# A batch-by-batch attention stage and an expert stage on one core: side work placed inside the first products, and the second product's tiles placed between the next unit's first products

## The chip, the cores and the metric

The kernel runs on one core of a Trainium2 chip. The metric is the device time of one execution in microseconds, less is better. The engines are named as in the profile: PE (TensorE) with its weight loads (PEld), DVE (VectorE), ACT (ScalarE), POOL (GpSimd) and SP (SyncE), each with its own queue of instructions, worked off in order.

## What is computed

For 16 batches of 256 positions and 256 channels (f32) the reference runs three residual blocks, each followed by a layer norm:

```python
x = layernorm(x + linear_recurrence(x))              # scan over positions, then a 256x256 product
x = layernorm(x + cross_attention(x, ctx))           # 16 heads of 16, rotary, window of 50
# experts:
probs = softmax over positions of (silu(h @ router_w1) @ router_w2).T      # 16 experts
weights, token_indices = top_k(probs, 64)            # each expert picks 64 positions of every batch
gate  = silu(picked @ w1[e]);  value = picked @ w2[e]
out   = (gate * value) @ w3[e]                       # scaled by the weights, scatter-added per batch
x = layernorm(x + combined)
```

Each expert has 256 channels in, 512 hidden (`FF`) and 256 out.

## The kernel before

The program has two blocks, each with an instruction stream per engine written out by hand, with semaphores between them.

**`mixing`** runs the recurrence, the attention and the router for one batch after another. A step of the pipeline (`step(it)`) has 16 slots `t`, one for each head; other stages of neighbouring batches are put into given slots. Step 15 is the last with heads; step 16 is a drain, with the last output projections. What matters here is the end: PE's output projection of batch 14 (`O`, L692) needs `attnT`, whose second half POOL makes in `inverse_sums(it, -1)` (L481 to L488) from ACT's `rough` (L826). In step 15 POOL also takes the first unit's token rows: it waits for `route.placed` (DVE, `place_picked`, L153), copies indices (L541) and issues four indirect DMAs (L545). PE turns these rows in step 16 (L726). After the projection come DVE's statistics (L953 to L962), ACT's estimate (L159, L161), POOL's refinement (L167 to L175), DVE's normalised rows `x2cur` (L969), PE's transposes (L657), ACT's copy `x2T` (L856), the router's first product (L740) and the last weighted sum of the attention (L636). All engines go to the second block together.

**`experts`** handles 32 units: 16 experts times two halves of the batches, each with four tiles of 128 rows (`CB` = 4, a tile holds the 64 picks of two batches). All products are split in three for accuracy (hi·hi, hi·lo, lo·hi in fp32r), so a unit costs PE:

- `up`: for each of four `f` tiles of the hidden size, six 128x512 products into `gate_bank` and six into `value_bank` (L1342). A bank pair alternates, so `f` waits for gate and hidden of `f - 2`.
- `turn`: eight transposes of the next unit's rows (L1352), which ACT and DVE split into `xT_hi` and `xT_lo` (`columns`).
- `down`: for four tiles `m`, twelve 128x256 products each into `y_bank` (L1342, `attn` in the trace), for the unit before. A bank pair alternates again.

Some names: `gate_of` (ACT, L1465), `multiply` (DVE, L1560), `h_high` (ACT, L1469), `h_low` (DVE, L1552) make the hidden operand; `split` (ACT L1452, DVE L1542) the weights; `weigh` (ACT, L1479) scales each output tile `y`; `gather` (POOL, L1265) fetches rows two units ahead; `scatter` (POOL, L1283) adds `y` to `acc_rows`, each tile after the same tile of the unit before has landed.

The last batch's rest is handled in the first units, with single-unit additions: `project_O` in unit 0, `normalise_O` (DVE, L1615) at the end of unit 2, `turn_x2` (PE, L1401), ACT's copy `x2T` (L1502), `route_x2` (L1408) and the copy to `r1` (L1513) in unit 3 (`LATE - 1`), POOL's preparation of `rw2_placed` (L1299, L1306), the logits (L1430) and `find_maximum` (L1644) in unit 4 (`LATE`), the turned picks (L1438) and `place_picked` (L153) in unit 10. PE's order in a unit is:

```python
turn_x2 (unit 3);  up(it);  turn(it.step(1));  side work of this unit, and its wait;  down(it.step(-1))
```

At the end DVE, ACT and POOL normalise the last four accumulators (`statistics(c)`, L1567; `normalise(c)`, L1578), each after its last scatter and a load.

Of the kernel before, what the change touches and what calls it, by code (L numbers as in the profile page):

```python
# [28 lines left out]
P = 128  # L29
NB = 16  # L30
S = 256
# [146 lines left out]
def mixing(nc, dram, keep):  # L178
# [5 lines left out]
    with ExitStack() as ctx:  # L184
# [260 lines left out]
        def _(pool):  # L445
# [54 lines left out]
            def step(it):  # L500
# [47 lines left out]
                if behind and not drain:  # L548
                    inverse_sums(it, -1)
# [565 lines left out]
def experts(nc, dram, keep):  # L1115
# [8 lines left out]
    with ExitStack() as ctx:  # L1124
# [70 lines left out]

        def has_next(it, d=1):
            return not it.fixed or it.i + d < UNITS

        @block.sync
        def _(sp):  # L1200
# [15 lines left out]
            def unit(it):  # L1216
# [29 lines left out]
        def _(pool):  # L1246
# [46 lines left out]
            def unit(it):  # L1293
# [4 lines left out]
                if it.is_unit(LATE):  # L1298
# [3 lines left out]
                if it.is_unit(LATE):  # L1302
# [32 lines left out]
        def _(pe):  # L1335
# [20 lines left out]
            def up(it):  # L1356
# [5 lines left out]
                for f in range(FT):  # L1362
                    if it.at_least(1) or f >= 2:
# [9 lines left out]
            def down(it):  # L1373
# [4 lines left out]
                for m in range(CB):  # L1378
# [31 lines left out]

            def unit(it):
# [9 lines left out]
                if it.is_unit(LATE - 1):  # L1421
                    route_x2()
                    pe.wait_ge(freed["R"], NB + FREED_EARLY)
                if it.is_unit(LATE):
                    pe.wait_ge(rw2_set, 1)
                    pe.wait_ge(y_scaled, it.lin(CB, -CB))
                    pe.wait_ge(silu_done, 1)
                    for c in range(GB):
                        b = GB + c
                        mm = nc.tensor.matmul(y_bank[0][:, 0:S], rw2_placed[:, c, :], r1[:, b * S:(b + 1) * S],  # L1430
                                              start=(c == 0), stop=(c == GB - 1))
                    mm.then_inc(logits_ready, 1)
                    pe.wait_ge(logits_kept, 1)
                if it.is_unit(LATE + 6):
                    pe.wait_ge(route.picked, 1)
                    pe.wait_ge(y_scaled, it.lin(CB, -CB))
                    for n, src in enumerate((route.token, route.weight)):
                        nc.tensor.transpose(y_bank[n][:, 0:P], src[:].rearrange("p a s -> p (a s)"),  # L1438
                                            ident[:]).then_inc(picked_turned, 1)
# [8 lines left out]
        def _(act):  # L1448
# [22 lines left out]
            def weigh(it):  # L1471

                for m in range(CB):
# [15 lines left out]
            def unit(it):  # L1489
# [3 lines left out]
                gate_of(it, 0)  # L1493
                split(it, 2)
                gate_of(it, 1)
                h_high(it, 0)
                if has_next(it):
                    split(it.step(1), 0)
                gate_of(it, 2)
# [3 lines left out]
                h_high(it, 1)  # L1503
                if has_next(it):
                    split(it.step(1), 1)
                gate_of(it, 3)
                h_high(it, 2)
                h_high(it, 3)
                if has_next(it):
                    columns(it.step(1))  # L1510
                if it.is_unit(LATE - 1):
                    act.wait_ge(ready["R"], NB)
                    nc.scalar.copy(r1[:, B * S:NB * S], y_bank[1][:, 0:S]).then_inc(freed["R"], 1)  # L1513
                if it.at_least(1):
                    weigh(it.step(-1))
# [22 lines left out]
        def _(dve):  # L1538
# [80 lines left out]
            def unit(it):  # L1619
                multiply(it, 0)  # L1620
                split(it, 2)
                multiply(it, 1)
                h_low(it, 0)
                if has_next(it):
                    split(it.step(1), 0)
                multiply(it, 2)
                h_low(it, 1)
                if has_next(it):
                    split(it.step(1), 1)
                multiply(it, 3)  # L1630
                h_low(it, 2)
                h_low(it, 3)
                if it.is_unit(LATE + 6):
                    dve.wait_ge(picked_turned, 2)
                    place_picked(dve, route, keep, slice(CB, NC2), y_bank)
                if has_next(it):
                    columns(it.step(1))
# [4 lines left out]
                if it.is_unit(LATE):  # L1642
                    dve.wait_ge(logits_ready, 1)
                    nc.vector.tensor_copy(route.p[:], y_bank[0][:, 0:S]).then_inc(logits_kept, 1)  # L1644
                    dve.wait_ge(logits_kept, 1)
                    find_maximum(dve, route, route.p[:])
# [117 lines left out]
```

## Time and profile before

| | |
|---|---|
| median of 3 runs | 1093.72 us (1092.81 to 1095.04) |
| the profiled execution's own time | 1093.0 us |
| its span in the profile | 1091.1 us |
| busy: PE, PEld, DVE, ACT, POOL | 91%, 78%, 67%, 54%, 64% |
| mean granted TensorE clock | 0.974 |
| stages | `mixing` to 482 us, units 0 to 31 from there to 1064 us, last normalisation to the end |

The page gives busy time of each engine, the granted clock and groups of instructions. The trace gives instructions in order of time, with the idle time before them and what ended it, stretch by stretch. A PE row's duration includes the array's pipeline, so that the spacing of starts, not the sum of durations, is the pace.

### The profile page before, as it was taken

The numbers are of one execution on the slowest core, as the hardware profiler recorded it, in microseconds if no ns is written. First come the engines' busy times: TensorE is split into PE (matmuls) and PEld (weight loads), VectorE is DVE, ScalarE is ACT, GpSimd is POOL, SyncE is SP. The second block draws the span as 40 slices with busy tenths as digits, with TensorE's granted clock in tenths as the row PEclk, the third lists the DMA queues.
The fourth block names the chain that finished last, engine by engine and source line by source line (L and its number), as shares of the span: only waits on it lengthen the run. The fifth ranks groups of instructions, "written<-read, shape, count | busy, mean of one in ns | idle before, by whom it ended". The sixth has DMA issues, their size and how long they took to land.

```text
span 1091.1 us, 21188 instructions
## 1 busy us (share of the span) xinstructions
PE 997.3 (91%) x6436; PEld 846.9 (78%) x6436; DVE 732.6 (67%) x2176; ACT 592.8 (54%) x1226; POOL 698.1 (64%) x785
## 2 busy tenths in 40 slices
PE   4699999999989998779989999999999999999990
PEld 3577778788777776558878898889888898889890
DVE  4678888887877887746654686565647665855634
ACT  1255566555575555546654656555656566655641
POOL 5556666666766565346765777676776767777543
PEclk8999999999999999889989999999999999999995
DMA  6344343433343333425674667566787666666746
GB/s 188 85 102 99 99 107 101 103 101 101 101 110 92 80 79 74 175 77 160 175 193 99 139 158 155 131 147 148 162 211 178 119 172 123 168 140 156 163 78 178
DMA packets 114998, 142.57 MB, mean 131 GB/s; under 512 B 15184, under 2 KB 88144, under 8 KB 114768
## 3 DMA queue, kind: packets, MB, share of 16 engines
q1 hardware_dynamic: 87600, 106.62, 34.4%
q0 software_dynamic: 24576, 33.57, 18.2%
q10 hardware_dynamic: 2720, 1.17, 0.5%
q8 instruction: 45, 0.74, 0.3%
q14 instruction: 57, 0.47, 0.1%
HBM read 90.71 MB, written 29.36 MB: 110 GB/s over the span
## 4 chain that ended last, share of the span: by engine, by line
PE 48%; DVE 2%; ACT 1%; POOL 1%; issue 1%; DMA 1%; DVEq 0%; POOLq 0%; SPq 0%; ACTq 0%
PE attn L1342 16%; PE gate_bank L1342 15%; PE value_bank L1342 15%; PE turn_bank L1352 2%; DMA acc_rows<-y,slots_now 1%; DMA last<-acc_rows 1%; PE attn L1430 0%; POOL acc_rows L1283 0%; POOL arena L1265 0%; DVE stats L1567 0%; DVE hidden L1560 0%; DVE last L1578 0%; DVE h_lo L1552 0%; ACT L1465 0%; ACT y L1479 0%
## 5 line engine op out<-in xcount | busy, mean ns | idle before, releaser
L1283 POOL DMA_INDIRECT acc_rows<-y,slots_now x128 | 201.7, 1576 | 127.3 <-ACT y L1479 98.2
L1560 DVE TENSOR_TENSOR hidden<-gate,value_bank 128x512 f32<-128x512 f32 x128 | 88.0, 688 | 196.7 <-ACT gate L1465 192.8
L787 ACT ACTIVATE probsT<-scoreT 128x356 f32<-128x356 f32 x256 | 117.7, 468 | 143.8 <-PE scoreT L618 119.5
L945 DVE CUSTOM_DVE_ANT_0 scored<-score,band 128x178 f32<-128x178 f32 x512 | 149.9, 337 | 62.0 <-PE score L589 57.9
L1465 ACT ACTIVATE gate<-gate_bank 128x512 f32<-128x512 f32 x128 | 76.7, 599 | 146.8 <-PE value_bank L1342 146.7
L1342 PE MATMUL attn<-w_hi,h_hi 128*128 128x256 f32 x512 | 147.4, 288 | 5.2 <-DVE weight_of L153 2.7
L1342 PE MATMUL attn<-w_hi,h_lo 128*128 128x256 f32 x512 | 143.7, 281 | 0.0
L1342 PE MATMUL attn<-w_lo,h_hi 128*128 128x256 f32 x512 | 143.7, 281 | 0.0
L589 PE MATMUL score<-k_stack,q_stack 96*128 96x178 f32 x512 | 123.4, 324 | 7.2 <-DVE nmax L945 4.4
L589 PEld LDWEIGHTS score<-k_stack,q_stack 96*128 96x128 f32 x512 | 88.7, 193 | 36.9 <-DVE nmax L945 16.8
L618 PE MATMUL scoreT<-q_stack,k_stack 97*128 97x356 f32 x256 | 116.7, 457 | 0.0
L1479 ACT ACTIVATE y<-attn,weight_of 128x256 f32<-128x256 f32 x128 | 61.1, 478 | 90.0 <-PE attn L1342 84.8
L1342 PEld LDWEIGHTS attn<-w_hi,h_hi 128*128 128x128 f32 x512 | 97.7, 191 | 6.4 <-DVE weight_of L153 3.0
L1265 POOL DMA_INDIRECT rows<-x_rows,rows_now x64 | 81.8, 1278 | 28.0 <-issue 14.6
L1342 PE MATMUL gate_bank<-k_stack,q_stack 128*128 128x512 f32 x384 | 97.9, 390 | 0.5 <-PEq L184 0.5
L1342 PE MATMUL value_bank<-k_stack,q_stack 128*128 128x512 f32 x384 | 97.5, 389 | 0.0
L1342 PEld LDWEIGHTS attn<-w_hi,h_lo 128*128 128x128 f32 x512 | 97.2, 190 | 0.0
L1342 PEld LDWEIGHTS attn<-w_lo,h_hi 128*128 128x128 f32 x512 | 97.1, 190 | 0.0
L1265 POOL DMA_INDIRECT arena<-x_rows,rows_now x60 | 72.8, 1214 | 26.9 <-issue 14.3
L1552 DVE TENSOR_TENSOR h_lo<-hidden,h_hi 128x512 fp32r<-128x512 f32 x128 | 87.9, 687 | 3.1 <-ACT h_hi L1469 0.3
L616 PE MATMUL scoreT<-band_bf,ident_bf 128*128 128x356 bf16 x256 | 83.9, 328 | 6.1 <-ACT probsT L787 3.9
L1542 DVE TENSOR_TENSOR w_lo<-arena,w_hi 128x1024 fp32r<-128x1024 f32 x64 | 79.6, 1244 | 12.5 <-ACT w_hi L1452 12.4
(213 smaller groups left out, 2422.1 us busy)
## 6 DMA issues: line engine op xcount, KB each, us to landing
arena<-in_w SPq DMA_DIRECT2D x96, 512.0 KB, 3.9
k_stack<-high_k SPq DMA_DIRECT2D x128, 64.0 KB, 2.2
q_stack<-high_q SPq DMA_DIRECT2D x128, 64.0 KB, 2.3
arena<-in_xT SPq DMA_DIRECT2D x16, 256.0 KB, 2.9
arena<-in_x SPq DMA_DIRECT2D x16, 256.0 KB, 3.1
arena<-in_cT SPq DMA_DIRECT2D x16, 256.0 KB, 3.7
k_stack<-low_k SPq DMA_DIRECT2D x64, 64.0 KB, 2.2
q_stack<-low_q SPq DMA_DIRECT2D x64, 64.0 KB, 2.2
```

What stands on the lines that cost most here:

```text
L589: mm = nc.tensor.matmul(score[t % 2][:, q * SPAN:(q + 1) * SPAN], q_stack[par][0:TOP, t // 2, t % 2, q * P:(q + 1) * P], k_stack[par][0:TO ...
L616: nc.tensor.matmul(out, ident_bf[:], band_bf[:, k, :].unsqueeze(1).to_broadcast([P, 2, SPAN]), start=True, stop=False)
L618: nc.tensor.matmul(out, k_stack[par][0:TOP + 1, f, k * P:(k + 1) * P], q_stack[par][0:TOP + 1, f, :, k * FIRST:k * FIRST + SPAN], start=Fa ...
L787: nc.scalar.activation(probsT[g % 2][:, u % HG, :, :].rearrange("p a s -> p (a s)"), scoreT[u % 2][:, 0:2 * SPAN], ACT.Exp, scale=1.0 / DH ...
L945: op = nc.vector.tensor_tensor_reduce(scored[t % 2][:, q, :], score[t % 2][:, q * SPAN:(q + 1) * SPAN], band[:, q, :], -1.0, BIG, ALU.add, ...
L1265: nc.gpsimd.indirect_dma_start(rows[it.par][:, m, :], None, dram["x2"][it.h], bass.IndirectOffsetOnAxis(ap=now[:, m:m + 1], axis=0)).then_ ...
L1283: nc.gpsimd.indirect_dma_start(dram["acc"][c], bass.IndirectOffsetOnAxis(ap=now[:, m:m + 1], axis=0), y[m][:], None, compute_op=ALU.add).t ...
L1342: mm = nc.tensor.matmul(out, a[x], b[z], start=(n == 1), stop=(n == 3 * len(pairs)))
L1465: nc.scalar.activation(gate[f % 2][:], gate_bank[f % 2][:], ACT.Silu).then_inc(gate_ready, 1)
L1542: nc.vector.tensor_tensor(w_lo[it.par][n][:], raw[n], w_hi[it.par][n][:], ALU.subtract).then_inc(w_lo_ready[n], 1)
L1552: nc.vector.tensor_tensor(h_lo[it.par][:, f, :], hidden[f % 2][:], h_hi[it.par][:, f, :], ALU.subtract).then_inc(h_lo_ready, 1)
L1560: nc.vector.tensor_tensor(hidden[f % 2][:], gate[f % 2][:], value_bank[f % 2][:], ALU.mult).then_inc(hidden_ready, 1)
```

## The change

Five edits.

1. In step 15 of `mixing` POOL runs `inverse_sums(it, -1)` before the wait for `route.placed` and the four row gathers.
2. `rw2` is loaded and placed in units 0 and 1, no longer in 3 and 4.
3. The side work on PE stands inside `up` (`aside`): in unit 0 `turn` of the next unit before the products of `f` = 3; in unit 3 `turn_x2` before `f` = 0 and `route_x2` before `f` = 2; the logits of unit 4 and the turned picks of unit 10 before `f` = 2. What ACT and DVE do with them is moved between their `f` steps too.
4. In all units but 0, 1, 3, 4 and 10 (`woven`) the four `down` tiles of the unit before stand between the `up` tiles: tile 0, `turn`, tile 1, then `f` = 2, tile 2, `f` = 3, tile 3. In the last unit tiles 2 and 3 follow `f` = 3.
5. ACT and DVE follow that order in the woven units.

The core of the diff:

```diff
@@ mixing, POOL, step
+                if behind and not drain:
+                    inverse_sums(it, -1)
                 if it.fixed and it.i == NB - 1:
                     pool.wait_ge(route.placed, 1)
...
-                if behind and not drain:
-                    inverse_sums(it, -1)
@@ experts
+        PLAIN = (0, 1, LATE - 1, LATE, LATE + 6)
+        def woven(it):
+            return not it.is_unit(*PLAIN)
@@ SP, unit
+                if it.is_unit(0):
+                    sp.dma_start(rw2[:], dram["rw2"]).then_inc(rw2_in, 16)
                 if it.is_unit(LATE - 1):
-                    sp.dma_start(rw2[:], dram["rw2"]).then_inc(rw2_in, 16)
@@ POOL, unit: memset of rw2_placed, and the wait for rw2_in with the eight copies
-                if it.is_unit(LATE):
+                if it.is_unit(1):
@@ PE, up
                 for f in range(FT):
+                    aside(it, f)
+                    if woven(it) and f == 2:
+                        down(it.step(-1), 0, 1)
+                        if has_next(it):
+                            turn(it.step(1))
+                        down(it.step(-1), 1, 2)
+                    if woven(it) and f == 3 and has_next(it):
+                        down(it.step(-1), 2, 3)
@@ PE, down
-            def down(it):
+            def down(it, first=0, end=CB):
...
-                for m in range(CB):
+                for m in range(first, end):
@@ PE, new
+            def aside(it, f):
+                if it.is_unit(0) and f == 3:
+                    turn(it.step(1))
+                if it.is_unit(LATE - 1) and f == 0:
+                    turn_x2(it)
+                if it.is_unit(LATE - 1) and f == 2:
+                    route_x2()
+                if it.is_unit(LATE) and f == 2:
+                    logits(it)
+                if it.is_unit(LATE + 6) and f == 2:
+                    turn_picked(it)
@@ PE, unit
-                if it.is_unit(LATE - 1):
-                    turn_x2(it)
                 up(it)
-                if has_next(it):
+                if has_next(it) and not it.is_unit(0) and not woven(it):
                     turn(it.step(1))
...
-                    down(it.step(-1))
+                    down(it.step(-1), (3 if has_next(it) else 2) if woven(it) else 0)
@@ ACT, unit, woven (DVE alike, see the order below)
+                    gate_of(it, 0)
+                    split(it, 2)
+                    gate_of(it, 1)
+                    h_high(it, 0)
+                    weigh(it.step(-1), 0, 1)
+                    if has_next(it):
+                        split(it.step(1), 0)
+                        columns(it.step(1))
+                    weigh(it.step(-1), 1, 2)
+                    h_high(it, 1)
+                    gate_of(it, 2)
+                    if has_next(it):
+                        split(it.step(1), 1)
+                        weigh(it.step(-1), 2, 3)
+                    h_high(it, 2)
+                    gate_of(it, 3)
+                    h_high(it, 3)
+                    weigh(it.step(-1), 3 if has_next(it) else 2)
```

In the other units ACT copies `x2T` before `gate_of(it, 0)` and `r1` before `gate_of(it, 2)` (unit 3), and DVE does `find_maximum` (unit 4) and `place_picked` (unit 10) before `multiply(it, 2)`. `normalise_O` stays behind the last `h_low` of unit 2.

POOL in step 15 of `mixing`, before:

```order
L541 COPY rows_now<-row_of 128x4 [waits route_placed0]
L545 DMA arena<-x_rows,rows_now 128x256 [waits x2_kept,rows_taken]
L545 DMA arena<-x_rows,rows_now 128x256 x3
L481 TENSOR_TENSOR inverse<-sums,rough 128x256 [waits rough_ready]
L484 TENSOR_SCALAR inverse<-inverse 128x256 [waits inverse_chain]
L486 TENSOR_TENSOR inverse<-inverse,rough 128x256 [waits inverse_chain]
L488 TENSOR_TENSOR attnT<-vals,inverse 128x256 [waits inverse_chain]
```

and now:

```order
L481 TENSOR_TENSOR inverse<-sums,rough 128x256 [waits rough_ready]
L484 TENSOR_SCALAR inverse<-inverse 128x256 [waits inverse_chain]
L486 TENSOR_TENSOR inverse<-inverse,rough 128x256 [waits inverse_chain]
L488 TENSOR_TENSOR attnT<-vals,inverse 128x256 [waits inverse_chain]
L543 COPY rows_now<-row_of 128x4 [waits route_placed0]
L547 DMA arena<-x_rows,rows_now 128x256 [waits x2_kept,rows_taken]
L547 DMA arena<-x_rows,rows_now 128x256 x3
```

The four steps that end in `attnT` now stand ahead of the copy and the four gathers.

DVE in the later part of unit 2 (`hidden` is `multiply`, `xT_lo` is `columns`, `x2cur` is `normalise_O`), before:

```order
L1560 TENSOR_TENSOR hidden<-gate,value_bank 128x512 [waits h_lo_ready,gate_ready]
L1552 TENSOR_TENSOR h_lo<-hidden,h_hi 128x512 [waits h_hi_ready]
L1542 TENSOR_TENSOR w_lo<-arena,w_hi 128x1024 [waits w_hi_ready1]
L1560 TENSOR_TENSOR hidden<-gate,value_bank 128x512 [waits h_lo_ready,gate_ready]
L1552 TENSOR_TENSOR h_lo<-hidden,h_hi 128x512 [waits h_hi_ready] x2
L1547 TENSOR_TENSOR xT_lo<-turn_bank,xT_hi 128x512 [waits xT_hi_ready] x2
L1615 TENSOR_SCALAR x2cur<-pre_O,mv_O,rstd_O 128x256 [waits rstd_ready_O,x2_kept]
```

and now:

```order
L1600 TENSOR_TENSOR xT_lo<-turn_bank,xT_hi 128x512 [waits xT_hi_ready] x2
L1605 TENSOR_TENSOR h_lo<-hidden,h_hi 128x512 [waits h_hi_ready]
L1613 TENSOR_TENSOR hidden<-gate,value_bank 128x512 [waits h_lo_ready,gate_ready]
L1595 TENSOR_TENSOR w_lo<-arena,w_hi 128x1024 [waits w_hi_ready1]
L1605 TENSOR_TENSOR h_lo<-hidden,h_hi 128x512 [waits h_hi_ready]
L1613 TENSOR_TENSOR hidden<-gate,value_bank 128x512 [waits h_lo_ready,gate_ready]
L1605 TENSOR_TENSOR h_lo<-hidden,h_hi 128x512 [waits h_hi_ready]
L1668 TENSOR_SCALAR x2cur<-pre_O,mv_O,rstd_O 128x256 [waits rstd_ready_O,x2_kept]
```

The column split has gone ahead of the third product's work, and `x2cur` still follows the fourth `h_lo`.

## Rows read from the trace of the kernel before

**Rows 1.** The page, part 1: busy time, share of the span and instructions of each engine.
```profile
PE 997.3 (91%) x6436; PEld 846.9 (78%) x6436; DVE 732.6 (67%) x2176; ACT 592.8 (54%) x1226; POOL 698.1 (64%) x785
```
**Rows 2.** Stretches: start:end, length, busy of PE, PEld, DVE, ACT, POOL, clock, DMA.
```profile
684.00:686.00 2.00, 1.58 (x13) 1.58 (x14) 1.65 (x5) 0.00 (x0) 0.00 (x0) 1.00 0.34 132
718.31:1000.32 282.01, 281.26 (x1666) 248.07 (x1665) 174.30 (x257) 166.54 (x277) 202.42 (x166) 1.00 0.68 157
```
**Rows 3.** Who waited for whom on PE, 380 us to the end.
```profile
PE work L692 <- POOL attnT L488: 6.6, 1, 6.6
PE attn L1430 <- POOL rw_placed L1306: 2.6, 1, 2.6
PE attn L1401 <- ACT y L1479: 0.7, 1, 0.7
```
**Rows 4.** Groups on PE from 482 us: busy, mean ns, idle before and releasers.
```profile
L1342 PE MATMUL attn<-w_hi,h_hi 128*128 128x256 f32 x512 | 147.4, 288 | 5.2 <-DVE weight_of L153 2.7 <-ACT r L1513 1.9 <-DVE p_route L1644 0.5
L1342 PE MATMUL gate_bank<-xT_hi,w_hi 128*128 128x512 f32 x128 | 50.9, 398 | 2.5 <-DVE xT_lo L1547 1.7 <-DVE hidden L1560 0.7
```
**Rows 5.** Timeline of ACT and POOL, steps 15 and 16, and POOL in unit 0.
```profile
454.12 0.42 ACT L826 ACTIVATE rough<-sums_log 128x256 f32<-128x256 f32 x1
...
456.77 1.90 POOL L545 DMA_INDIRECT arena<-x_rows,rows_now  x1 [0.71 <-POOL rows_now L541]
...
462.18 0.95 POOL L545 DMA_INDIRECT arena<-x_rows,rows_now  x1 [0.30 <-issue]
463.16 0.73 POOL L481 TENSOR_TENSOR inverse<-sums,rough 128x256 f32<-128x256 f32 x1
...
465.38 0.72 POOL L488 TENSOR_TENSOR attnT<-vals,inverse 128x256 f32<-128x256 f32 x1
...
487.75 1.80 POOL L1318 TENSOR_TENSOR inverse<-sums,rough 128x256 f32<-128x256 f32 x1
...
492.16 1.12 POOL L1325 TENSOR_TENSOR attnT<-vals,inverse 128x256 f32<-128x256 f32 x1
```
**Rows 6.** Timeline of PE, step 16 up to the second block.
```profile
466.25 2.04 PE L692 MATMUL work<-wo,attnT 128*128 128x256 f32 x4 [6.60 <-POOL attnT L488]
...
476.98 0.66 PE L657 MATMUL work<-ident,x2cur 128*128 128x128 f32 x4 [1.19 <-DVE x2cur L969]
...
482.08 1.62 PE L1342 MATMUL gate_bank<-k_stack,q_stack 128*128 128x512 f32 x6 [0.50 <-PEq L184]
```
**Rows 7.** Timeline of PE and DVE at the end of unit 2.
```profile
526.11 1.04 PE L1352 MATMUL turn_bank<-ident,rows 128*128 128x128 f32 x8
...
527.54 1.46 DVE L1552 TENSOR_TENSOR h_lo<-hidden,h_hi 128x512 fp32r<-128x512 f32 x2
...
530.12 0.73 DVE L1615 TENSOR_SCALAR x2cur<-pre_O,mv_O,rstd_O 128x256 f32<-128x256 f32 x2
```
**Rows 8.** The chain that ended last, units 3 to 6: start, us, what.
```profile
548.72 7.37 PE attn L1342 x48
...
570.50 5.14 PE attn L1430 x16
576.15 5.73 PE attn L1342 x48
...
593.74 5.63 PE attn L1342 x48
599.37 1.38 PE gate_bank L1342 x6
600.75 1.36 PE value_bank L1342 x6
```
**Rows 9.** Timeline of POOL and DVE, last units and after.
```profile
1056.61 1.57 POOL L1283 DMA_INDIRECT acc_rows<-y,slots_now  x1 [8.79 <-ACT y L1479]
...
1064.82 1.57 POOL L1283 DMA_INDIRECT acc_rows<-y,slots_now  x1 [0.86 <-ACT y L1479]
...
1073.34 1.41 DVE L1567 BATCH_NORM_STATS2 stats<-last 128x6 f32<-128x256 f32 x4 [17.25 <-DMA last<-acc_rows]
```

More of the change, by code:

```diff
@@ L1301, in unit @@
                     gather(it.step(2))
-                if it.is_unit(LATE):
+                if it.is_unit(1):
                     pool.wait_ge(rw2_zeroed, 1)
@@ L1469, in h_high, with weigh @@
                 nc.scalar.copy(h_hi[it.par][:, f, :], hidden[f % 2][:]).then_inc(h_hi_ready, 1)
-            def weigh(it):
-                for m in range(CB):
+            def weigh(it, first=0, end=CB):
+                for m in range(first, end):
                     act.wait_ge(y_ready, it.lin(CB, m + 1))
@@ L1492, in unit @@
                     nc.scalar.activation(half, half, ACT.Silu).then_inc(silu_done, 1)
[L1493 to L1499, printed above, removed]
                 if it.is_unit(LATE - 1):
@@ L1502, in unit @@
                     nc.scalar.copy(x2T[:].rearrange("p k s -> p (k s)"), y_bank[0][:]).then_inc(freed["OX"], 1)
[L1503 to L1513, printed above, removed]
@@ L1514, in unit @@
-                if it.at_least(1):
-                    weigh(it.step(-1))
+                if woven(it):
+                    gate_of(it, 0)
[16 more added lines that the diff above has]
+                    weigh(it.step(-1), 3 if has_next(it) else 2)
+                else:
+                    gate_of(it, 0)
+                    split(it, 2)
+                    gate_of(it, 1)
+                    h_high(it, 0)
+                    if has_next(it):
+                        split(it.step(1), 0)
+                    if it.is_unit(LATE - 1):
+                        act.wait_ge(ready["R"], NB)
+                        nc.scalar.copy(r1[:, B * S:NB * S], y_bank[1][:, 0:S]).then_inc(freed["R"], 1)
+                    gate_of(it, 2)
+                    h_high(it, 1)
+                    if has_next(it):
+                        split(it.step(1), 1)
+                    if it.is_unit(0):
+                        columns(it.step(1))
+                    gate_of(it, 3)
+                    h_high(it, 2)
+                    h_high(it, 3)
+                    if has_next(it) and not it.is_unit(0):
+                        columns(it.step(1))
+                    if it.at_least(1):
+                        weigh(it.step(-1))
@@ L1619, in unit @@
             def unit(it):
[L1620 to L1635, printed above, removed]
@@ L1636, in unit @@
-                if has_next(it):
-                    columns(it.step(1))
+                if woven(it):
+                    multiply(it, 0)
+                    split(it, 2)
+                    multiply(it, 1)
+                    h_low(it, 0)
+                    if has_next(it):
+                        split(it.step(1), 0)
+                        columns(it.step(1))
+                    h_low(it, 1)
+                    multiply(it, 2)
+                    if has_next(it):
+                        split(it.step(1), 1)
+                    h_low(it, 2)
+                    multiply(it, 3)
+                    h_low(it, 3)
+                else:
+                    multiply(it, 0)
+                    split(it, 2)
+                    multiply(it, 1)
+                    h_low(it, 0)
+                    if has_next(it):
+                        split(it.step(1), 0)
+                    if it.is_unit(LATE):
+                        dve.wait_ge(logits_ready, 1)
+                        nc.vector.tensor_copy(route.p[:], y_bank[0][:, 0:S]).then_inc(logits_kept, 1)
+                        dve.wait_ge(logits_kept, 1)
+                        find_maximum(dve, route, route.p[:])
+                    if it.is_unit(LATE + 6):
+                        dve.wait_ge(picked_turned, 2)
+                        place_picked(dve, route, keep, slice(CB, NC2), y_bank)
+                    multiply(it, 2)
+                    h_low(it, 1)
+                    if has_next(it):
+                        split(it.step(1), 1)
+                    if it.is_unit(0):
+                        columns(it.step(1))
+                    multiply(it, 3)
+                    h_low(it, 2)
+                    h_low(it, 3)
+                    if has_next(it) and not it.is_unit(0):
+                        columns(it.step(1))
```

34 lines of the change are left out of this document (15 added, 19 removed).

## The prediction

> **What bounds the kernel now.** I read the page first: PE is busy 91% of the span, no other engine over 67% [rows 1]. So I looked for where PE isn't busy, by stretches. In the middle of the expert stage nothing is left: between 718 and 1000 us PE is busy 281.26 of 282.01 us at full clock, 16 units of 17.6 us, while DVE, ACT and POOL are busy 174, 167 and 202 us [rows 2]. The reader is to see there that tiles moved between tiles can give nothing back in the steady part. Then the waits of PE. They are few and single: 6.6 us for `attnT` at the end of the attention stage [rows 3]; in the expert stage 2.7 us for `place_picked` (unit 10), 1.9 for the router's copy (unit 3), 0.5 for the maximum's copy (unit 4), 1.7 for `xT_lo` (unit 1) and 0.7 for a late `hidden` (unit 23) [rows 4], and 2.6 for `rw2_placed` (unit 4) and 0.7 for the last `y` before `turn_x2` (unit 3) [rows 3]. Last the chain and the timelines around them, for what a wait drags behind it.
>
> **The change, part by part.**
>
> *Step 15.* ACT's `rough` is there at 454.54. POOL's four steps took 463.16 to 466.10, 2.94 us, only because the gathers of 456.77 to 463.13 stood ahead [rows 5]. Moved ahead they end at about 457.5, and PE, which came to the projection at 459.65 (466.25 less its 6.60 of waiting) [rows 6], finds `attnT` ready: the 6.6 us go. The drain behind was 10.7 us from there to `turn` of x2 (466.25 to 476.98) and 5.1 more to the first unit (482.08) [rows 6]. In its first part the projection's four products took 2.04 us, at half clock after the idle time; without idle time before it I take 1.4 us less for the drain's first part. What comes late next are the rows: the gathers start 1.7 us later and end at about 464.8; landing is not shown, and I take 2 us. PE reaches their transposes at about 465.5 and waits some 1.3, but `x2cur` isn't there before 468.5, so that it is hidden. Sum 8.0 us. Bounds: 5, if the rows land late and push what follows, and 9.5, if the whole drain speeds up.
>
> Against the 2.94 us stands a second row: the same four steps took 5.53 us in unit 0 (487.75 to 493.28), with DVE busy beside them [rows 5]. In the new place DVE is busy too (picks, then a weight split). With 5.53 `attnT` is ready at 460.1, PE waits 0.5 and the rows land at 469.4, which costs 2 us of the 8. I take 2.94 since in step 15 itself, next to the same stream, such a chain took 0.7 us a step. The Trainium skill (GPSIMD Engine Reference, Key points) says that GpSimd shares its SBUF interfaces with VectorE and contends with instructions that have two SBUF inputs; the slower row agrees with it. By the skill's rule the term would be 6, by mine 8.
>
> *Unit 0.* `turn` of unit 1 goes ahead of `f` = 3, so `xT_lo` is ready when `up` of unit 1 starts: 1.7 us go [rows 4]. Cover: its gather's last issue ended at about 487.7, and `turn` now comes 8.2 us after 482.08, at 490.3. With 2 us of landing this just holds. The early `rw2` work puts about 3.5 us more on POOL in unit 1, ahead of `scatter(0)`, which then waits under 1 us longer; nobody waits for it.
>
> *Unit 2 to unit 3.* This one costs. In unit 2 `x2cur` follows the last `h_low`. The last up product ended at 526.11, `h_low` at 529.00, and `x2cur` takes 0.73 [rows 7]: without `xT_lo` between them it is ready 3.6 us after the products. PE had 6.6 us of turns and `down` tiles as cover; in the woven unit one `down` tile is left, 5.73/4 = 1.4 us [rows 8]. `turn_x2` stands at the head of unit 3, so PE waits 2.2 us where it waited 0.7 [rows 3]: +1.5 us, and I count 1.6 with the semaphores. It would be nothing if `x2cur` stood earlier.
>
> *Unit 3.* `x2T` and `route_x2` are inside `up`; the 1.9 us go [rows 4], and the half clock after them, in which the `down` tiles took 7.37 us against 5.73 and 5.63 [rows 8]: 1.5. Together 3.4 us.
>
> *Unit 4.* The waits of 2.6 and 0.5 go [rows 3, 4]. The logits took 5.14 us at half clock [rows 8]; at full clock half of it, 2.4 to 2.6 less. Against it, `down` ran slightly faster after a wait. Sum 5.4 us. Cover for the logits: `rw2_placed` is two units old, the SiLU of `r1` runs at the unit's start.
>
> *Unit 10.* The 2.7 us for the placed picks go [rows 4], less 0.3, as products behind a wait ran faster than in the steady part: 2.4 us.
>
> *Unit 23.* `hidden` was late because ACT loaded tables at the end of unit 22. Now a `down` tile, `turn` and another tile stand ahead of `f` = 2, 3.6 us of cover: 0.9 us with what trailed it.
>
> *The woven units, 27 of 32.* The same instructions. I walked the waits of one unit: `f` = 2 needs a gate and `hidden` that are over 4 us old, the next unit's `f` = 1 needs this unit's last `hidden`, which is ready 1.5 us after its product while PE has one `down` tile and one `f` tile (4.1 us) to do: 2.6 us of slack, the smallest. ACT's queue (10.4 us of 17.6) now waits for `y` in the middle, with `h_high` behind it, but `down` needs that only a unit later. POOL's scatters start earlier and spread. So zero. Bounds: an `f` group behind a `down` tile took 1.38 us against 1.36 [rows 8], and there are four more changes of kind a unit: 27 x 4 x 0.02 = 2 us slower. Other way, undisturbed tiles ran a few per cent faster, so up to 4 us could come back if the neighbours' work falls better.
>
> *The tail.* The last unit now has two `down` tiles of unit 30 before its `f` = 2. POOL's eight scatters in a row, 1.87 us apart from 1056.61 [rows 9], lose two: its last products end 2.7 us later than before, so tile 2 is issued at about 1059.3 and tile 3 at 1061.2, the first of unit 31 at 1063.8 (2.6 us later, as 1064.82 came after 1062.2) instead of 1064.82. The first statistics (1073.34) follow it by 8.5 us, and DVE's chain follows those. PE needs the last `h_low` 2.8 us after the products and gets it after 2.9 [rows 7]. Gain 1.0 us; bounds 0 and 1.9.
>
> **Sum:** 8.0 + 1.7 - 1.6 + 3.4 + 5.4 + 2.4 + 0.9 + 1.0 = 21.2 us. Against the profiled execution's own 1093.0 that is 1071.8. The median of the runs shown is 1093.72, 0.7 above it; I forecast **1072.5 us** for the median.
>
> **Rivals.**
>
> *Half clock at the new wait (0.28).* After the waits of 6.6, 1.9 and 2.6 us the products ran at half clock, as their lengths show (2.04, 7.37 and 5.14 us) [rows 6, 8]; after the 2.7 us wait of unit 10 the granted clock stayed at 1.00 [rows 2]. The new wait of 2.2 us lies among them. If it falls, `turn_x2` and the first products of unit 3 pay what the tiles did after the 1.9 us wait, 1.6 us up to the 2.5 of the logits: 1074 to 1075. The Trainium skill (TensorE: Matmul & The Clock Gate, Part 1) says that the array is slow until activity releases it, and that the point at which it changes differs from run to run; that 2.7 us kept the clock here and 1.9 us lost it fits.
>
> *The drain is bound by latency (0.2).* Its steps are single instructions on five engines, and the rows land behind the later gathers. Then only 4 to 6 of the 8 us come, with the slow POOL chain as the likeliest reason: 1075 to 1077.
>
> *The change of kind between tiles costs PE (0.04, slower).* Place: each woven unit, where `f` groups of 512 columns, transposes and tiles of 256 columns now alternate, with a wait at each of them. If every one of the 108 added changes cost more than 21.2/108 = 0.20 us, the kernel would be slower; at 0.3 us it is 1104. Against it: the measured step after a tile is 0.02 us. For it: only that ACT's `weigh` now waits in the midst of the `f` work, a queue that the old order never held up.
>
> *The weave gives something (0.1).* If spread work on ACT, DVE and POOL lets products run nearer to the pace after waits (5.63 against the steady spacing of some 5.7), 27 units give 2 to 4 us: 1069.
>
> **Numbers.** The forecast has 0.38. The range takes in the half clock, the short drain and the better weave, and on the low side a drain of 9.5 with a tail of 1.9: 1067 to 1079. About 0.2 is left out, mostly above. Some 0.2% is what a measurement of this kernel can tell from no change. Slower by more than that is the one rival, 0.04; 0.01 is for a smaller form of it that ends near the time before; faster by more is the rest, 0.95.
>
> **What would show it.** Right: no `attnT` wait in step 16, the first unit's product near 473.5 on the trace's scale, no waits of `rw_placed`, `weight_of`, `r` and `xT_lo` on PE, one wait for `x2cur` of about 2.2 us ahead of unit 3, woven units of 17.5 to 17.7 us, first scatter of unit 31 closer to the end of PE by 1 us. Wrong: woven units above 17.8 us, a PE wait in each of them, or a new wait for the rows in the drain that moves the first unit's start past 476.

## The result, and the profile after

The changed kernel takes 1073.53 us (median of 4, 1073.45 to 1075.47) against 1093.26 us beside it: ratio 0.9821, 95% interval 0.9804 to 0.9838, some 1.8% less. The prediction was 1072.5 (1067 to 1079). The profiled span went from 1091.1 to 1071.5 us, 19.6 us.

Page, part 1, against [rows 1]:

```profile
PE 994.0 (93%) x6436; PEld 846.8 (79%) x6436; DVE 732.3 (68%) x2176; ACT 587.6 (55%) x1226; POOL 674.4 (63%) x785
```

PE's busy time is nearly the same; the span shrank around it. Who waited for whom on PE from 380 us on, against [rows 3] and [rows 4] (in total, times, longest):

```profile
PE score L726 <- DMA arena<-x_rows,rows_now: 2.6, 1, 2.6
...
PE attn L1416 <- DVE x2cur L1668: 2.2, 1, 2.2
```

The waits for `attnT`, `rw_placed`, `weight_of`, `r`, `p_route`, `xT_lo` and `hidden` have no row any more. Two new ones stand in their place: the gathered rows in the drain, and `x2cur` ahead of unit 3.

The drain, timelines of ACT, POOL and PE (against [rows 5, 6]):

```profile
455.34 0.42 ACT L826 ACTIVATE rough<-sums_log 128x256 f32<-128x256 f32 x1
...
455.84 0.72 POOL L481 TENSOR_TENSOR inverse<-sums,rough 128x256 f32<-128x256 f32 x1 [4.17 <-ACT rough L826]
...
458.05 1.59 POOL L488 TENSOR_TENSOR attnT<-vals,inverse 128x256 f32<-128x256 f32 x1
...
460.07 2.24 POOL L547 DMA_INDIRECT arena<-x_rows,rows_now  x1 [0.30 <-POOL rows_now L543]
...
465.13 0.95 POOL L547 DMA_INDIRECT arena<-x_rows,rows_now  x1 [0.30 <-issue]
```

```profile
460.71 1.03 PE L692 MATMUL work<-wo,attnT 128*128 128x256 f32 x4
...
467.85 1.18 PE L726 MATMUL score<-ident,arena 128*128 128x128 f32 x8 [2.63 <-DMA arena<-x_rows,rows_now]
...
469.55 1.42 PE L636 MATMUL attn<-probsT,vp 128*32 128x178 f32 x16
470.90 1.12 PE L657 MATMUL work<-ident,x2cur 128*128 128x128 f32 x4
```

From the start of `rough` to the first unit the kernel before took 27.96 us (454.12 to 482.08) and this one 21.24 (455.34 to 476.58), 6.7 us less. `rough` itself came 1.2 us later, with nothing changed ahead of it; over all profiles here it started between 451.6 and 456.5 us. The last gather landed 2.7 us after its issue began (465.13 to 467.85), and the wait for it brought half clock: the sixteen products of L636 took 1.42 us, 0.81 at full. So no more than the old wait was gained: from the projection's first product (L692) to the first unit the kernel before took 15.83 us (466.25 to 482.08) and this one 15.87.

The start of each unit (its first gate product) in this kernel:

```profile
476.58 0.47 PE L1349 MATMUL gate_bank<-k_stack,q_stack 128*128 128x512 f32 x1 [0.50 <-PEq L184]
...
490.10 0.51 PE L1349 MATMUL gate_bank<-xT_hi,w_hi 128*128 128x512 f32 x1
...
507.73 0.40 PE L1349 MATMUL gate_bank<-k_stack,q_stack 128*128 128x512 f32 x1
...
527.99 0.47 PE L1349 MATMUL gate_bank<-xT_hi,w_hi 128*128 128x512 f32 x1
...
546.43 0.40 PE L1349 MATMUL gate_bank<-k_stack,q_stack 128*128 128x512 f32 x1
...
567.38 0.40 PE L1349 MATMUL gate_bank<-xT_hi,w_hi 128*128 128x512 f32 x1
```

The same in the kernel before, from unit 1 on:

```profile
497.59 0.50 PE L1342 MATMUL gate_bank<-xT_hi,w_hi 128*128 128x512 f32 x1 [1.74 <-DVE xT_lo L1547]
...
515.20 0.39 PE L1342 MATMUL gate_bank<-k_stack,q_stack 128*128 128x512 f32 x1
...
533.84 0.48 PE L1342 MATMUL gate_bank<-xT_hi,w_hi 128*128 128x512 f32 x1
...
555.91 0.40 PE L1342 MATMUL gate_bank<-k_stack,q_stack 128*128 128x512 f32 x1
...
581.71 0.39 PE L1342 MATMUL gate_bank<-xT_hi,w_hi 128*128 128x512 f32 x1
```

A unit's length below is the distance of two such starts. With the same reading of the kernel before, the whole account is:

| term | forecast | before, us | after, us | gained |
|---|---|---|---|---|
| drain, from `rough` to the first unit | 8.0 | 27.96 | 21.24 | 6.7 |
| unit 0 | 1.7 | 15.51 | 13.52 | 2.0 |
| unit 2 (with the wait ahead of unit 3) | -1.6 | 18.64 | 20.26 | -1.6 |
| unit 3 | 3.4 | 22.07 | 18.44 | 3.6 |
| unit 4 | 5.4 | 25.80 | 20.95 | 4.9 |
| unit 10 | 2.4 | 20.45 | 17.96 | 2.5 |
| unit 23 | 0.9 | 18.62 | 17.59 | 1.0 |
| the other 24 units from 5 to 30 | 0 | 17.550 each | 17.532 each | 0.4 |
| from unit 31's start to the end | 1.0 | 49.11 | 47.80 | 1.3 |
| sum | 21.2 | | | 20.8 |

Less the 1.2 us by which `rough` came later, that is the 19.6 us of the spans. The steady part in one stretch, against [rows 2] (start:end, length, busy of PE, PEld, DVE, ACT, POOL, clock, DMA), PE busy in all of it (281.26 of 282.01 us before):

```profile
700.00:970.00 270.00, 270.00 (x1599) 238.87 (x1598) 168.27 (x250) 156.99 (x268) 186.37 (x159) 1.00 0.66 158
```

The tail on POOL, against [rows 9]:

```profile
1040.91 1.56 POOL L1290 DMA_INDIRECT acc_rows<-y,slots_now  x1 [5.24 <-ACT y L1510]
1042.78 1.56 POOL L1290 DMA_INDIRECT acc_rows<-y,slots_now  x1 [0.30 <-ACT y L1510]
...
1045.40 1.58 POOL L1290 DMA_INDIRECT acc_rows<-y,slots_now  x1 [0.86 <-ACT y L1510]
```

Only two scatters of unit 30 are left before the first of unit 31, which starts 21.7 us after unit 31's first product (1023.70) instead of 22.8 (1041.99 to 1064.82). It is 21.7 in all eight profiles with the weave and 22.8 or 22.9 in all five without; from that scatter to the end the profiles differ by 1.1 us (25.8 to 26.9).

### The profile page after: what moved, and what is told of

It reads as the page before. It is cut to its first block, busy times and chain, and to the rows that moved or that the text cites. A ratio compares the mean times of both kernels' runs of the same rounds, so it can differ in the third digit from the quotient of the medians.

```text
span 1071.5 us, 21268 instructions
## 1 busy us (share of the span) xinstructions
PE 994.0 (93%) x6436; PEld 846.8 (79%) x6436; DVE 732.3 (68%) x2176; ACT 587.6 (55%) x1226; POOL 674.4 (63%) x785
## 4 chain that ended last, share of the span: by engine, by line
PE 52%; DVE 1%; DMA 1%; issue 1%; ACT 0%; POOL 0%; DVEq 0%; POOLq 0%; SPq 0%; ACTq 0%
PE gate_bank L1349 16%; PE attn L1349 16%; PE value_bank L1349 16%; PE turn_bank L1359 2%; DMA last<-acc_rows 1%; DVE stats L1620 0%; DMA acc_rows<-y,slots_now 0%; DVE last L1631 0%; PE attn L1433 0%; DVE hidden L1613 0%; PE attn L1406 0%; ACT y L1510 0%; ACT h_hi L1500 0%; DVE mv L1624 0%; ACT w_hi L1483 0%
## 5 line engine op out<-in xcount | busy, mean ns | idle before, releaser
L1290 POOL DMA_INDIRECT acc_rows<-y,slots_now x128 | 205.6, 1606 | 136.5 <-issue 73.4
L618 PE MATMUL scoreT<-q_stack,k_stack 97*128 97x356 f32 x256 | 117.0, 458 | 0.0
L1605 DVE TENSOR_TENSOR h_lo<-hidden,h_hi 128x512 fp32r<-128x512 f32 x128 | 88.3, 690 | 22.6 <-ACT h_hi L1500 21.7
L1272 POOL DMA_INDIRECT rows<-x_rows,rows_now x64 | 78.0, 1219 | 28.0 <-issue 14.3
L1500 ACT CAST h_hi<-hidden 128x512 fp32r<-128x512 f32 x128 | 78.8, 616 | 23.4 <-DVE hidden L1613 23.1
L1272 POOL DMA_INDIRECT arena<-x_rows,rows_now x60 | 70.8, 1180 | 26.9 <-issue 14.0
```

The source lines that it names most:

```text
L618: nc.tensor.matmul(out, k_stack[par][0:TOP + 1, f, k * P:(k + 1) * P], q_stack[par][0:TOP + 1, f, :, k * FIRST:k * FIRST + SPAN], start=Fa ...
L1272: nc.gpsimd.indirect_dma_start(rows[it.par][:, m, :], None, dram["x2"][it.h], bass.IndirectOffsetOnAxis(ap=now[:, m:m + 1], axis=0)).then_ ...
L1290: nc.gpsimd.indirect_dma_start(dram["acc"][c], bass.IndirectOffsetOnAxis(ap=now[:, m:m + 1], axis=0), y[m][:], None, compute_op=ALU.add).t ...
L1500: nc.scalar.copy(h_hi[it.par][:, f, :], hidden[f % 2][:]).then_inc(h_hi_ready, 1)
L1605: nc.vector.tensor_tensor(h_lo[it.par][:, f, :], hidden[f % 2][:], h_hi[it.par][:, f, :], ALU.subtract).then_inc(h_lo_ready, 1)
```

## The experiments

**The step 15 edit, undone and alone.** Both kernels move one call:

```diff
# a_inverse_back: the changed kernel, with
-                if behind and not drain:
-                    inverse_sums(it, -1)
                 ...
+                if behind and not drain:
+                    inverse_sums(it, -1)
# b_inverse_only: the kernel before, with the opposite
```

> The changed kernel with its step 15 edit undone: the four gathers ahead of the four steps to attnT again. Theory 1 (each part of the gain belongs to one named wait): the 6.6 us wait for attnT is back, the wait of 2.6 us for the rows at their transposes is gone, the first unit starts about 6 us later than in the changed kernel, all units and the tail unchanged: 1079 to 1081 us. Theory 2 (the drain's pace is set by single steps on five engines, and the order on POOL matters little, the later start of the stages before is what is seen): under 3 us later, 1074 to 1076 us.

> The kernel before with the step 15 edit alone. Theory 1: the first unit's start comes 5.5 to 6.7 us earlier, with a new wait of 2 to 3 us for the gathered rows at L726 and half clock behind it; everything from unit 0 on as before: 1087 to 1088 us. Theory 2: within 3 us of before, 1090 us or more.

a: 1079.21 us (ratio to before 0.987, 0.9841 to 0.9899), b: 1085.34 us (0.9924, 0.9898 to 0.995). PE in the drain, of a and then of b:

```profile
465.67 2.04 PE L692 MATMUL work<-wo,attnT 128*128 128x256 f32 x4 [6.61 <-POOL attnT L488]
```

```profile
464.17 1.97 PE L726 MATMUL score<-ident,arena 128*128 128x128 f32 x8 [2.68 <-DMA arena<-x_rows,rows_now]
...
473.85 0.94 PE L1342 MATMUL gate_bank<-k_stack,q_stack 128*128 128x512 f32 x3 [0.50 <-PEq L184]
```

Here a's time is in the range of theory 1 (1079 to 1081) and b's is 1.7 us under it (1087 to 1088). From `rough` to the first unit a takes 28.23 us and b 22.23, as theory 1 has it. In b the half clock began at the rows themselves (1.97 us for the eight, 1.18 in the changed kernel), which cost it 1 us. The profiled run of b (1081.94 us) is 3.4 us under its median, and its trace shows how a single run can come out so low: `rough` came at 451.62, and unit 3 took 20.45 us and unit 4 24.59, against 22.07 and 25.80 before, with the same code and the same waits of 1.89 and 2.65 us. The clock did not fall behind them. What made the median 1.7 us less than expected isn't shown, since only this run has a trace.

**Without the weave.**

```diff
         def woven(it):
-            return not it.is_unit(*PLAIN)
+            return False
```

> The changed kernel with woven() false for every unit: the side work of units 0, 3, 4 and 10 stays inside the first products, all second-product tiles are behind them. Theory 1 (the weave hides nothing in the steady part): the 2.2 us wait for x2cur ahead of unit 3 falls to 0.7 (for y), unit 22 takes about 1 us more again, the tail 1.2 us more, the units on average 17.58 instead of 17.53 us (1.2 us over 25 units): in sum +1.5 to +2.5 us, 1075 to 1076 us. Theory 2 (the weave is what makes the kernel faster, since ACT, DVE and POOL no longer come in bursts): 1082 us or more. Theory 3 (the change of kind between tiles costs PE time): units shorter without the weave, time below 1073.

1072.94 us (0.9805, 0.9782 to 0.9828): no difference from the changed kernel that the runs can tell (one of 1070.31, one of 1074.05). The time that theory 1 gave, 1075 to 1076, was missed by 2 us. The trace has the waits that it named: unit 2 takes 18.64 us again, and the old wait is back in unit 23,

```profile
888.03 0.47 PE L1349 MATMUL gate_bank<-xT_hi,w_hi 128*128 128x512 f32 x1 [0.75 <-DVE hidden L1613]
```

which makes that unit 18.63 us; the 24 steady units take 17.559 each (17.532 woven), unit 0 14.02 (13.52), and from unit 31 to the end it is 48.95 (47.80). So the weave gives 1.0 us in unit 23 and 1.2 in the tail, and takes 1.6 back in unit 2: 0.6 us net, which the medians can't tell from nothing. The other two differences aren't the weave's as far as is shown: the steady units of the kernels without it took 17.533 (run g) to 17.559 us, and unit 0, which isn't woven, took 13.99 to 14.37 us in five of the later profiles of woven kernels. Theory 2 falls. Theory 3's time, below 1073, was just met, but not its ground: no unit is shorter without the weave by more than 0.05 us, apart from unit 2, whose wait is known.

**The early `rw2` alone, on the kernel before.**

```diff
-                if it.is_unit(LATE - 1):
+                if it.is_unit(0):
                     sp.dma_start(rw2[:], dram["rw2"]).then_inc(rw2_in, 16)
...
-                if it.is_unit(LATE):          # memset, and the eight copies
+                if it.is_unit(1):
```

> The kernel before with the early load and placing of rw2 alone (units 0 and 1 instead of 3 and 4). Theory 1: of the 5.4 us of unit 4 the wait of 2.6 us goes, and the logits run at full clock if the clock fell for that wait alone (5.1 to about 2.7 us); the 0.5 us wait for p_route stays: unit 4 is 4.5 to 5.2 us shorter, about 1088.5 us. Rival: the wait moves to the next thing that the logits need (the SiLU, or y): less than 2 us shorter.

1089.88 us in its one run. Unit 4 takes 21.47 us, 4.3 less than before (4.5 to 5.2 were expected; the rival's less than 2 falls):

```profile
566.16 3.62 PE L1431 MATMUL attn<-r,rw_placed 128*128 128x256 f32 x16
```

The wait is gone. The logits take 3.6 us at full clock, not the 2.7 that was expected: the 5.14 of before were only partly at half clock (it lasted from 570.0 to 573.4 us). And unit 10, untouched, took 23.31 us instead of 20.45, behind the same wait of 2.73 us. The clock there (start:end, length, busy, clock before the last two columns), first this kernel, then the one before:

```profile
680.00:682.00 2.00, 2.00 (x12) 2.00 (x11) 0.00 (x0) 0.47 (x1) 0.00 (x0) 0.50 0.00 0
```

```profile
686.00:688.00 2.00, 2.00 (x20) 2.00 (x19) 0.00 (x0) 0.95 (x2) 0.51 (x1) 1.00 0.00 0
```

The same code, the same wait: once 12 products in 2 us, once 20.

**The new wait ahead of unit 3.** First the cause, then what stands behind it:

```diff
# d_x2_earlier, DVE, unit
                     h_low(it, 2)
+                    if it.is_unit(2):
+                        normalise_O()
                     multiply(it, 3)
...
-                if it.is_unit(2):
-                    normalise_O()
# i_x2_and_y: the same, and PE, turn_x2
-                pe.wait_ge(y_scaled, it.lin(CB, -CB))
+                pe.wait_ge(y_scaled, it.lin(CB, -CB - 1))
```

> The changed kernel with normalise_O in unit 2 ahead of the fourth multiply instead of behind the fourth h_low. Theory 1 (x2cur is what turn_x2 waits 2.2 us for, and the last y is next): the wait becomes about 1.0 us, for ACT's y, unit 2 takes 19.0 instead of 20.26 us. Rival: the fourth hidden, pushed back 0.7 us by it, delays something else in unit 3, and the two units together get less than 0.6 us shorter.

> As the run before, and turn_x2 waits for the y of all but the last tile, since it writes the other bank. Theory 1: no wait ahead of unit 3, unit 2 takes 18.0 us, 2.2 us less than in the changed kernel. Rival: the wait only moves to unit 3's route_x2 or to the copy x2T on ACT, behind the last y, and units 2 and 3 together keep over 1 us of it.

d, one run of 1074.34 us:

```profile
527.68 0.52 PE L1416 MATMUL attn<-ident,x2cur 128*128 128x128 f32 x3 [1.11 <-ACT y L1510]
```

Unit 2 takes 19.15 us. i, one run of 1069.89 us: no wait there, unit 2 17.85 us, 2.4 less than 20.26, unit 3 18.46 (18.44 in the changed kernel). Both rivals fall: units 2 and 3 together are 1.1 us shorter in d and 2.4 in i. One run's time says nothing here (d came out above the changed kernel: its first unit started 0.6 us later, and unit 0 took 0.6 and the tail 0.8 us more); the units do.

**The rows' wait, by moving PE's work.**

```diff
-                    if only(it, NB, t, 5):
+                    if only(it, NB, t, 6):
                         pe.wait_ge(rows_in[0], 16 * CB)
```

> The changed kernel with PE's transposes of the gathered rows (L726) one slot later in step 16, behind the transposes of x2cur. Theory 1 (the 2.6 us wait for the rows holds up x2cur's transposes by 1.8 us and brings half clock): from rough (L826) to the first unit's start 21.2 us become 18.5 to 19.5 us; the wait at the rows is gone. Rival: x2cur's chain and the split of the rows behind it on DVE set the first unit's start, and the gain is under 0.7 us.

This missed. 1077.62 us in one run; from `rough` to the first unit 22.88 us, 1.6 more than in the changed kernel:

```profile
469.21 1.11 PE L657 MATMUL work<-ident,x2cur 128*128 128x128 f32 x4 [1.19 <-DVE x2cur L969]
470.12 1.91 PE L726 MATMUL score<-ident,arena 128*128 128x128 f32 x8
...
474.38 2.07 PE L740 MATMUL work<-x2T,rw 128*128 128x256 f32 x4 [1.14 <-ACT x2T L856]
```

and ACT:

```profile
472.66 0.47 ACT L787 ACTIVATE probsT<-scoreT 128x356 f32<-128x356 f32 x1 [3.75 <-PE scoreT L618]
...
473.74 0.59 ACT L856 COPY x2T<-work 128x512 f32<-128x512 f32 x1
```

The transposes of `x2cur` did start 1.8 us earlier after `rough` (13.79 us, 15.56 in the changed kernel), as theory 1 said. But from 468.1 us on everything ran at half clock, up to the first unit's start:

```profile
471.00:474.00 3.00, 2.24 (x9) 1.45 (x7) 2.58 (x4) 1.34 (x4) 0.22 (x1) 0.50 0.25 87
474.00:477.00 3.00, 2.62 (x15) 1.58 (x19) 0.00 (x0) 1.07 (x3) 0.00 (x0) 0.50 0.00 0
```

The theory left out two things. One is ACT's queue: the copy `x2T` stands there behind `probsT`, which needs a `scoreT` product (L618), and that one still stands behind the rows' transposes on PE. From the start of `x2cur`'s transposes to that product's start it was 3.3 us now (469.21 to 472.52) and 1.4 in the changed kernel (470.90 to 472.33), so that the lead of 1.8 us was gone and the router's product began no earlier (18.96 us after `rough`, 18.87 there). The other is the clock: it stretched the rows' transposes within these 3.3 us (1.91 us; 1.09 at full clock in run h below), and from the router's product to the first unit it took 3.9 us instead of 2.4. The second part is the 1.6 us that the run lost. What the edit does at full clock wasn't tried in another run.

**The rows' wait, by freeing POOL.**

```diff
-                    for n, (i, at) in enumerate(((NB - 1, 13), (NB, 0))):
+                    for n, (i, at) in enumerate(((NB, 0), (NB, 1))):
```

> The changed kernel with DVE's two weight splits at the end of the attention stage (L1060) moved from (step 15, slot 13) and (step 16, slot 0) to (step 16, slots 0 and 1), away from POOL's chain to attnT. Theory 1 (POOL's fourth step took 1.59 instead of 0.73 us and the first gather 2.24 because DVE read SBUF beside it): the four steps take 2.9 to 3.0 us, the last gather is issued 1 to 1.5 us earlier after rough, and the wait for the rows is about 1.5 us instead of 2.6. Rival: the gather's 2.24 us have another cause, the chain is 0.9 us faster and the rows' wait falls by that at most.

POOL, then PE:

```profile
459.19 0.73 POOL L488 TENSOR_TENSOR attnT<-vals,inverse 128x256 f32<-128x256 f32 x1
460.35 1.99 POOL L547 DMA_INDIRECT arena<-x_rows,rows_now  x1 [0.30 <-POOL rows_now L543]
...
465.17 0.95 POOL L547 DMA_INDIRECT arena<-x_rows,rows_now  x1 [0.30 <-issue]
...
467.98 1.09 PE L726 MATMUL score<-ident,arena 128*128 128x128 f32 x8 [1.42 <-DMA arena<-x_rows,rows_now]
...
470.78 0.66 PE L657 MATMUL work<-ident,x2cur 128*128 128x128 f32 x4 [0.65 <-DVE x2cur L969]
```

From `rough` to the first unit 19.41 us, 1.8 less, and the drain kept its clock. The fourth step of the chain takes 0.73 us instead of 1.59 with the split out of its way. The wait for the rows is 1.4 us, as theory 1 has it, and 1.2 less than in the changed kernel, more than the rival allows. The first gather still takes 1.99 us (2.24 in the changed kernel), but this does not speak for another cause, since the splits now stand right beside it. DVE in the changed kernel, and then in this run:

```profile
457.60 1.45 DVE L1060 TENSOR_TENSOR q_stack<-arena,q_stack 128x1024 fp32r<-128x1024 f32 x1
...
460.02 1.21 DVE L1060 TENSOR_TENSOR q_stack<-arena,q_stack 128x1024 fp32r<-128x1024 f32 x1
```

```profile
460.05 2.36 DVE L1060 TENSOR_TENSOR q_stack<-arena,q_stack 128x1024 fp32r<-128x1024 f32 x2
```

In every profile the drain's gathers beside such a split took 1.65 to 2.24 us and the others 0.94 to 0.97, also in the kernel before, where it was the first two (1.90, 1.66) [rows 5]. That the split is the cause is likely from this and not shown: no run has both splits behind the gathers, and in the expert stage some gathers beside a split of DVE kept their length (0.95 us for the one at 486.77 in the kernel before). Unit 3 of this run took 19.97 us instead of 18.44: here the clock did fall behind the 2.3 us wait for `x2cur`. The run's 1075.53 us comes from that, from a late `rough` (456.47) and from 0.9 us more in unit 0.

**All repairs, with and without the weave, and the changed kernel beside them.** k is the changed kernel with the edits of i and h; l the same repairs with `woven` false; m the changed kernel as it is.

> The changed kernel with the three repairs that worked: normalise_O ahead of the fourth multiply of unit 2, turn_x2 waiting for all y but the last, DVE's two weight splits in step 16, slots 0 and 1. Theory 1 (waits in different places add up): from rough to the first unit 19.4 us instead of 21.2, unit 2 17.9 instead of 20.3, all else as in the changed kernel: 4.2 us less in the trace, 1069 to 1070 us. Rival (the clock falls at other places instead, as it did when the rows were turned later): under 2.5 us less, 1071 us or more.

> The same repairs with woven() false for every unit (there normalise_O can stay at the end of unit 2). With no wait for x2cur to pay, Theory 1 gives the weave its whole worth: unit 22 to 23 about 1.0 us, unit 0's rows and steady units 0.7, the tail 1.2 us, so 2.5 to 3 us more than the run before: 1072 to 1073 us. Theory 2 (the weave is worth more where nothing else waits): over 4 us more. Theory 3 (it is worth nothing): within 1 us.

> The changed kernel unchanged, as the measure for the two runs beside it on the same chip: 1073 to 1074 us; its drain 21.2 us from rough to the first unit, unit 2 20.3 us. If the clock falls at the wait for x2cur, unit 3 takes about 20 us instead of 18.44.

| | median, us | ratio to before, 95% | `rough` to unit 0 | unit 2 | unit 31 to the end |
|---|---|---|---|---|---|
| k | 1068.84 | 0.9769 (0.9749 to 0.9789) | 18.93 | 17.84 | 47.75 |
| l | 1071.21 | 0.9799 (0.9777 to 0.9821) | 18.92 | 17.80 | 49.00 |
| m | 1073.06 | 0.9802 (0.978 to 0.9825) | 21.33 | 20.26 | 48.23 |

k is 4.2 us under m, where the two terms in the traces make 4.8 (2.4 in the drain, 21.33 to 18.93, and 2.4 in unit 2, 20.26 to 17.84), and 2.4 under l, where the traces have 1.0 in the units and 1.25 in the tail. Each of k's five runs (1067.36 to 1068.95) lies under each of l's (from 1070.52) and of m's (from 1070.66), so k is the fastest version of this case. Between l and m the runs show no order: their intervals overlap, and so do their times. Of the expectations, those of theory 1 hold within 0.2 us for k (1069 to 1070) and within 0.8 for l (1072 to 1073); the rivals (1071 or more for k, over 4 us or within 1 us between k and l) fall. PE's waits in k from 455 to 1060 us, all that are over 0.5:

```profile
PE score L726 <- DMA arena<-x_rows,rows_now: 1.5, 1, 1.5
PE work L740 <- ACT x2T L856: 1.4, 1, 1.4
```

## Why the prediction was right

The way to the time was right: where PE's queue has no gap, reordering gives nothing, and each named wait is worth its length plus what the clock does behind it. That the sum came out to 0.4 us (20.8 for 21.2) is in part luck: the drain and unit 4 gave 1.8 us less than forecast, and six small terms together 1.4 us more, of which those of unit 0 and the tail vary by as much between profiles. One sign that the prediction named for its being wrong even came true as written, "a new wait for the rows in the drain that moves the first unit's start past 476": the wait is there, and the start is 476.58. The late `rough` is 1.2 us of it; without it the start would be 475.4, against 474.1 by the forecast's own sum.

- *Step 15*: forecast 8.0, measured 6.7. The step that failed is that the wait for the rows "is hidden" behind `x2cur`. Counted from the start of `rough`, so that the drift drops out, the rows landed after 12.5 us (467.85) where the forecast had 12.7 (466.8), and `x2cur` was complete after 13.8 (469.09) where it had 14.4 (468.5). Neither was late. But PE came to the rows 1.5 us sooner than forecast and waited 2.6 us, not 1.3; behind the rows' transposes stand a `scoreT` product and L636, which the forecast left out, and they ran at half clock. So `x2cur`'s transposes began 1.8 us after `x2cur` was complete. The term "POOL's four steps took 2.94 us" was mis-sized too: they took 3.80 (455.84 to 459.64), since the fourth ran beside a split of DVE, as run h shows. It cost nothing against the forecast, because the second gather took 0.97 us where the old row had 1.66: the gathers ended 10.7 us after `rough`, as forecast. With short four steps and full clock (run h) the drain is 19.41 us, 0.5 under the forecast's 19.96. The Trainium skill (GPSIMD Engine Reference, Key points) names contention with VectorE instructions that have two SBUF inputs, and the fourth step agrees (1.59 us, 0.73 with the split moved away). The 6 us that the prediction put beside it come from the 5.53 us row, not from the page, and the measured 6.7 does not confirm them, since the loss came another way. The rival of a drain bound by latency (4 to 6 of the 8 us) wasn't far: 6.7 lies between it and the forecast.
- *Unit 0*: 2.0 for 1.7. In most later runs the gather's landing was 0.2 to 0.4 us late and the unit took up to 14.4 us instead of 13.5, so that the cover "just holds" was too kind.
- *Unit 2 to 3*: -1.6 as forecast, and the wait of 2.2 us for `x2cur` to a tenth. Runs d and i show both things it was made of.
- *Unit 3*: 3.6 for 3.4. *Unit 10*: 2.5 for 2.4. *Unit 23*: 1.0 for 0.9. *Tail*: 1.3 for 1.0.
- *Unit 4*: 4.9 for 5.4. The step that failed is "at full clock half of it": the sixteen logit products take 3.6 us at full clock (run g), so 1.5 were to gain, not 2.5.
- *The woven units*: 0.4 us over 24 of them, for 0, which is within what the kernels without the weave differ by (17.533 to 17.559 us a unit). The alternation costs nothing that could be seen. The rival by which every change of kind costs PE 0.2 us falls with the table and run c: unwoven units are not shorter.
- *The half clock at the new wait*: it didn't happen in the changed kernel's profile, nor in a or m; it did in h and in e. There units 2 and 3 took 40.3 and 40.2 us together, 1.5 more than the 38.7 of the changed kernel, and the prediction had 1.6 for it. Two of five agree with a chance of 0.28 as well as so few can. The changed kernel has two profiles, and another wait in them, at 317 us, shows that one kernel can go either way (see the last section). The Trainium skill (TensorE: Matmul & The Clock Gate, Part 1) says that the point at which activity releases the clock differs from run to run. What differs in these traces is whether a wait brings the clock down, which is near to that and not the same.

## What to carry to other kernels

When one engine is busy all through the steady part, look only at its single waits, and price each as its length plus the half-clock stretch that may follow it; one more piece of work between a result and its user removes it. Before moving a piece of work, look which other engine's queue waits for what stands behind it: in run e that undid the gain. When work is woven in, ask which late result used the old block as cover: here one wait of 2.2 us came back, and moving the producer ahead of one instruction and loosening one semaphore count removed it. And compare runs by stretches between fixed events, since a start that drifts by 5 us hides terms of 1 or 2.

## What the runs showed of the hardware

- The same wait in the same code had different prices. Behind 2.73 us of idle time in unit 10, PE ran at full clock in one profile and at half in another, 2.9 us apart. Behind 1.89 us in unit 3 it was 22.07 us for the unit and 20.45. All 13 profiles have an idle time of 2.68 us at some 317 us, where no kernel differs; the clock fell behind it in one alone, that of the changed kernel, and not in m, which is the same kernel. The wait in the changed kernel, the stretch behind it there, and the same stretch in m:

```profile
320.41 0.32 PE L616 MATMUL scoreT<-band_bf,ident_bf 128*128 128x356 bf16 x1 [2.68 <-ACT probsT L787]
```

```profile
322.00:325.00 3.00, 3.00 (x25) 1.81 (x23) 1.73 (x6) 1.60 (x5) 2.60 (x5) 0.50 0.46 105
```

```profile
319.50:322.50 3.00, 2.65 (x27) 1.69 (x26) 2.26 (x10) 2.21 (x7) 2.58 (x5) 1.00 0.43 98
```

- From 100 us to the tail, a single idle time of 1.74 us or less was never followed by half clock in these profiles. In run e two in close order, 1.52 and 1.19 us, were.
- POOL's 128x256 product with a split of DVE beside it that reads two operands (L1060) took 1.59 us, and 0.73 with the split moved away.
- The four indirect gathers landed 2.7 to 2.8 us after the last one's issue began (465.13 to 467.85; 465.17 to 467.98).
